# Counting masks in a threshold search: folds of 512 columns and sums of 512 values in place of 256

## The reference

```python
        S = jax.nn.relu(att[:, 0])
        S = S.at[..., 0].set(0.0)
        S = S * (1.0 - jnp.eye(T, dtype=S.dtype))
        S_shifted = jnp.concatenate([jnp.zeros((B, 1, T), S.dtype), S[:, :-1]], axis=1)
        FF = jnp.cumsum(S_shifted, axis=1)
        att = att - FF[:, None]
        ratio = _pruning_ratio(T)
        memory_budget = max(1, int(T * ratio))
        if ratio < 1.0:
            FF_mod = jnp.where(causal[None], FF, jnp.inf)
            sorted_idx = jnp.argsort(FF_mod, axis=-1)
            rank = jnp.argsort(sorted_idx, axis=-1)
            eff_k = jnp.minimum(memory_budget - 1, i + 1)
            keep = rank < eff_k[None, :, None]
```

## Time and profile before

| what | value |
|---|---|
| median of three runs | 2983.0 us (2960.94 to 2986.77) |
| span of the profiled execution | 2972.6 us |
| search stage, first mask to last settling | 144.5 to 394.8 us |
| PE busy in the span | 2648.6 us (89%) |
| DVE busy | 1845.0 us (62%) |
| ACT busy | 1787.0 us (60%) |
| POOL busy | 337.1 us (11%) |
| folds, L887 | 2176 matmuls, 238.4 us busy |
| counts, L897 | 416 activations, 157.6 us busy, and 416 reads of the accumulator, 81.9 us |

### The profile page before, as it was taken

How to read it: one execution, slowest core, us unless ns; L and a number is a source line. 1 busy time by engine, 2 the same in 40 slices (tenths; PEclk the granted TensorE clock), 3 DMA queues, 4 the chain that set the end, 5 groups by cost and what they waited for, 6 DMA issues and landing times. The chain is left out here.

```text
span 2972.6 us, 75835 instructions
## 1 busy us (share of the span) xinstructions
PE 2648.6 (89%) x31084; PEld 1645.1 (55%) x31084; DVE 1845.0 (62%) x5185; ACT 1787.0 (60%) x3488; POOL 337.1 (11%) x710
## 2 busy tenths in 40 slices
PE   8998978888888799999998889999999999897596
PEld 3386955666666563222212456676676667655355
DVE  5599978778787574100001657777777787753862
ACT  2375856555566527999998227666666666532331
POOL 1100033222222010000000100000000000016016
PEclk8998979999999899999999899999999999898598
DMA  3140001001110202110000010000000000203103
GB/s 95 42 67 1 2 2 17 17 17 17 17 17 10 54 1 66 54 45 1 1 1 1 17 40 2 7 7 7 2 7 7 7 2 2 79 29 47 33 13 59
DMA packets 84736, 67.84 MB, mean 23 GB/s; under 512 B 40584, under 2 KB 73496, under 8 KB 84008
## 3 DMA queue, kind: packets, MB, share of 16 engines
q1 hardware_dynamic: 75944, 56.70, 8.0%
q0 software_dynamic: 8448, 6.30, 1.6%
HBM read 47.21 MB, written 19.96 MB: 23 GB/s over the span
## 5 line engine op out<-in xcount | busy, mean ns | idle before, releaser
L1733 ACT ACTIVATE arena<-ps 128x1024 f32<-128x1024 f32 x512 | 474.1, 1300 | 25.9 <-PE ps L1683 24.1
L1184 DVE CUSTOM_DVE_ANT_0 arena<-ps,arena 128x1024 f32<-128x1024 f32 (+7 forms) x384 | 349.7, 930 | 107.8 <-PE ps L1060 91.9
L2111 DVE CUSTOM_DVE_ANT_0 arena<-ps,arena 128x512 f32<-128x512 f32 (+3 forms) x640 | 371.2, 643 | 26.7 <-PE ps L1975 25.9
L1136 ACT ACTIVATE arena<-ps 128x1024 f32<-128x1024 f32 (+3 forms) x320 | 275.4, 895 | 133.4 <-PE ps L1093 129.9
L2068 ACT ACTIVATE arena<-arena 128x1152 f32<-128x1152 f32 (+15 forms) x256 | 306.4, 1199 | 63.4 <-DVE arena L2111 63.4
L1975 PE MATMUL ps<-arena 64*128 64x512 f32 (+3 forms) x1280 | 270.4, 547 | 3.5 <-ACT arena L2044 1.1
L1694 PE MATMUL ps<-arena 128*32 128x512 f32 x2048 | 273.0, 604 | 0.0
L2006 PE MATMUL ps<-arena 128*64 128x128 f32 x4352 | 262.3, 275 | 0.0
L2006 PEld LDWEIGHTS ps<-arena 128*64 128x64 f32 x4352 | 235.3, 137 | 33.4 <-issue 28.7
L887 PE MATMUL ps<-arena 128*128 128x256 bf16 (+1 forms) x2176 | 238.4, 273 | 14.7 <-DVE arena L859 9.3
L1088 PE MATMUL ps<-arena 64*128 64x64 f32 x4352 | 218.0, 232 | 19.4 <-ACT arena L1136 11.5
(11 more groups left out here) (298 smaller groups left out, 4095.0 us busy)
## 6 DMA issues: line engine op xcount, KB each, us to landing
arena<-scr_q SPq DMA_DIRECT2D x256, 32.0 KB
scr_s<-scr_f SPq DMA_DIRECT2D x1, 4096.0 KB, 17.7
arena<-scr_k SPq DMA_DIRECT2D x32, 128.0 KB
arena<-by_head_k SPq DMA_DIRECT2D x16, 192.0 KB
arena<-scr_s SPq DMA_DIRECT2D x16, 192.0 KB, 2.6
arena<-by_head_q SPq DMA_DIRECT2D x28, 96.0 KB
by_head_k<-arena SPq DMA_DIRECT2D x5, 512.0 KB, 4.5
scr_x<-arena SPq DMA_DIRECT2D x2, 1024.0 KB, 5.4
```

Of the source, the lines that this page charges most:

```text
L1136: e.activation(turned_block(u, kc), src, ACT.Exp, scale=-1.0).then_inc(exped, 1)
L1184: e.tensor_tensor_reduce(scored_block(u, g)[:, lo:hi], PS[:, 1024 * (k % 2):1024 * (k % 2) + hi - lo], NF[t][:, lo:hi], -1.0, mxs[:, col - ...
L1733: e.activation(PTR[k % RS], PS[:, at(n):at(n) + 1024], ACT.Sigmoid, scale=float(1 / np.sqrt(8.0))).then_inc(weighed, 1)
L2111: e.tensor_tensor_reduce(slot(u, t, g)[:, lo:hi], PS[:, base(step) + 512 * g:base(step) + 512 * g + hi - lo], bias, -1.0, mxs[:, col - 1:c ...
```

## The change

PE folds a mask in pieces of 512 columns onto a whole PSUM bank. ACT sums all 512 values of the bank. The junk areas become four of 256 words in place of eight of 128, on the same 1024 words, and ACT waits for its own count four back in place of eight back.

```diff
-            junk = [reg(2048 + 128 * i, 128).bitcast(BF16) for i in range(8)]
+            junk = [reg(2048 + 256 * i, 256).bitcast(BF16) for i in range(4)]
@@ search_tensor
-                    for c0 in range(0, W, 256):
-                        c1 = min(c0 + 256, W)
+                    for c0 in range(0, W, 512):
+                        c1 = min(c0 + 512, W)
                         m = e.matmul(bank(n % 8, c1 - c0), IDB, tally[n % 7][:, c0:c1], start=(c0 == 0), stop=(c1 == W))
@@ search_scalar
-                    if n >= 8:
-                        w.wait_ge(counted, n - 7)
-                    e.activation(junk[n % 8], bank(n % 8, 256), ACT.Copy, accum_out=cnt[:, s:s + 1]).then_inc(counted, 1)
+                    if n >= 4:
+                        w.wait_ge(counted, n - 3)
+                    e.activation(junk[n % 4], bank(n % 8), ACT.Copy, accum_out=cnt[:, s:s + 1]).then_inc(counted, 1)
```

## The result

The changed kernel takes 2985.57 us in the median of 20 runs (2974.92 to 2997.03); the kernel before, over 20 runs, 2972.01 us (2960.94 to 2999.44). The ratio is 1.0039, with a 95% interval of 1.0021 to 1.0057: **slower by 0.4%**, small but clear. The forecast of 2997 us was built on the three runs then shown, whose median of 2983.0 lies 11 us above that of twenty.

What follows compares the result with a forecast made beforehand. PE was taken to bound the search before, ACT after, at 7.54 us a round in place of 7.10; 12.8 + 0.8 + 0.6 + 0.2 = +14.4 us on a median of 2983 gave 2997 us, range 2976 to 3014.

Steps and rivals of the forecast that it cites:

- The bound before: In the search, PE sets the round of 7.10 us: 6.93 of columns plus 2.5 ns for each of 68 matmuls.
- The count: ACT's sum of 512 folded values at L897: 0.365 + 0.215 = 0.58 us, 13 of them 7.54 us a round.
- The sum: All added time in the search: 12.8 + 0.8 + 0.6 + 0.2 = +14.4 us, or 0.48%.
- 29 rounds: Full-clock rounds of the search, 14 and 15, each going from 7.10 to 7.54 us: +12.8 us.
- the stretch between the halves: Search from 251.15 to 284.96 us: nothing while DVE sets the pace, then 0.6 us for counts queueing after half clock.
- counted already: After the half-clock stretch before 284 us, the later settling was taken as included elsewhere, leaving 0.6 us there.
- The size that can be told: Whole kernel: about 1% (30 us) can be told from no change; same 0.85, slower 0.12, faster 0.03.
- The base: Whole kernel before: median of 2983.0 us, to which 14.4 us was added for 2997 us.
- A, the clock: PE's granted clock falls in the search because PE waits each round; five half-clock rounds give 3029 us; chance 0.07.
- B, PE stays the bound: In the search a count costs under 0.540 us, so the round is PE's 7.02 us: 2981 us; chance 0.08.
- C, a stall: ACT stalls at each set in the search; with 0.5 us of stall a round of 8.06 us: 3013 us; chance 0.05.
- What would show each step: Signs in the search: 264 us long, 597 ns activations, PE gap some 0.5 us, L843 waits about 22 us, clock 1.00.

Runs made afterwards that it cites:

- without tile 3: Kernel before, with tile 3 left unfolded and its mask summed by ACT straight from its buffer, and four junk areas: a round of 6.885 us, ratio 0.9995.
- the second comparison: The changed kernel run again, against the kernel before on the same chip: median of 12 runs 2985.04 us, ratio 1.0036 (1.0011 to 1.0061).
- the padding: Four more small DVE operations, results unused, ahead of each settling of the first set; added to the changed kernel: a round of 7.521 us.
- the padded kernel before: Kernel before with four more small DVE operations, results unused, ahead of each settling of the first set: a round of 7.122 us.

## Why the prediction was right and where it was wrong

**The bound before: right.** PE's 7.10 us as 6.93 of columns plus 2.5 ns for each matmul gave 7.02 for folds of 512, 7.04 for 448 and 6.885 without tile 3; the runs have 7.026, 7.044 and 6.885. The 0.2 to 0.3 us that DVE was said to have left in a round of 7.10 are 0.28: its round is 6.82 us in the run where it is the bound.

**The count: right.** 0.58 us and a round of 7.54 were forecast from plain activations of the same widths; 0.5785 and 7.52 were measured. The Trainium skill, "ScalarE: Activation LUTs", section "What ACT_TABLE_LOAD costs", gives 0.833 ns an element, and the step from 480 to 512 columns agrees, 0.83. The estimate by its fixed cost and its overlap of neighbours, 0.52 us for a count of 512, does not fit: 0.5785 was measured.

**The sum: right, with one term too small.** In the trace: first round 7.93 in place of 7.16 us, +0.8 (forecast 0.8); 29 rounds +12.1 (12.8); the stretch between the halves, 254.37 to 289.08 in place of 251.15 to 284.96, +0.9 (0.6); the tail 3.47 in place of 3.25, +0.2 (0.2). Together +14.0 where +14.4 was forecast. The round, 7.52 in place of 7.54 us, makes 0.7 of the difference with the rounding of 7.10, and the middle gives 0.3 back. There I had counted only the queue of counts after the half-clock stretch and called the later settling "counted already". It is not. DVE's long products take the same time in both kernels, 251.15 to 276.98 us before and 254.37 to 280.21 after, 25.8 us; they start from one settling and end ahead of another, so the 0.2 us by which a wide count settles later are paid once more. The rows of the changed kernel:

```profile
286.62 0.60 ACT L897 ACTIVATE arena<-ps 128x512 bf16<-128x512 f32 x1
...
288.35 0.61 ACT L897 ACTIVATE arena<-ps 128x512 bf16<-128x512 f32 x1
```

Three steps of 0.58 us, and 0.73 from the last start to the settling at 289.08. In the kernel before, the same three steps took 0.39 each (283.29 to 284.46) and the settling followed 0.50 us later, at 284.96. Together that is 0.8 us; the other 0.1 is that the first of the four counts starts 6.41 us behind the settling at 280.21, where it was 6.31.

**The size that can be told: wrong.** This is the step that failed. The prediction said that about 1%, 30 us, is what a measurement of this kernel can tell from no change, and so gave "same" 0.85 and "slower" 0.12, although its own sum stood at +14.4 us. It was right that the change lies within 1%. But it took the spread of single runs, 26 us, for what a comparison of many runs can tell. With 20 runs of each kernel the interval is 0.18% to either side, about 5 us and not 30, and 1.0021 to 1.0057 excludes no change; so does the second comparison, 1.0011 to 1.0061. The mechanism and the sum held, and by them the outcome to name was "slower", by a little; the 0.80 on rounds of 7.3 to 7.9 us, 7 to 25 us of loss, belonged there. The chances also differ within themselves: a tenth of the forecast was said to lie beyond 1%, and 0.05 of it stands in the sum.

**The base: wrong.** The absolute time was 11.4 us too high, and 11.0 of it is the median of three runs, 2983.0, in place of 2972.0. The profiled span of 2972.6 lay nearer, and span plus sum, 2987.0, is within 1.5 us of the measured median. That is luck in part: a profiled execution is one run like any other, and that of the run with tiles 3 and 4 summed directly, repeated, took 2953.95 us where the median of its 12 was 2968.04. So is it luck that the medians differ by 13.6 us, as near to 14.4 as that: their interval is 5 us wide to either side. What bears the mechanism out is the search in the traces, 14.0 us longer.

**The rivals.** *A, the clock:* out. PE stood 0.32 us in each round and the granted clock was 1.00 in every stretch of full rounds. The Trainium skill, "TensorE: Matmul & The Clock Gate", section "A second HAM failure mode: psum-queue depth-cycling", tells of short idles between bf16 matmuls of 512 columns that made the clock swing. This trace does not agree: from 150 to 254 us and from 290 to 402 us, with folds of that form over eight banks, the clock stayed at 1.00. *B, PE stays the bound:* out at 512, but it is what happens at 448 columns. *C, a stall:* out by the padding, which cost the changed kernel nothing, and by ACT's record, which has no idle time in full rounds.

**What would show each step.** The signs came in but for two of their numbers. PE's gap in a round is 0.32 us in the record, not 0.5; the record has PE busy for 7.20 us where its matmuls need 7.03, so 0.2 of the gap is hidden. And the activations of 512 columns, forecast at 597 ns, are recorded with 0.60 us only at the start of a half, and with up to 1.52 later; the last section tells why that is no cost. L843's waits rose to 23.2 us, 22 forecast. The claim that nothing outside the search moves by more than 5 us held in the pair (3.4 and 0.7), but it held by luck: in the second trace of the changed kernel the part ahead was 12.3 us shorter than in the kernel before and the part behind 10.3 longer.

## What to carry to other kernels

Before work is handed from a full engine to one with room, set the three needs of a round side by side: here PE 7.10, DVE 6.82, ACT 4.75 us. The change took 0.08 from the first and put 2.8 on the last, and the crossing, some 466 columns by an estimate from the 0.365 us of a count and the slope of plain activations, lies between the runs of 448 and 480. It could be worked out before any run. The same room on ACT, spent on whole tiles that PE then need not fold, shortened the round by 0.28 us. And when a change is worth a few tenths of a per cent, take the base from many runs, and ask what many runs can tell before "no change" is forecast.

## What the runs showed of the hardware

**ACT's records grow while it is the bound.** In the changed kernel an activation of 512 columns is recorded with 0.60 us at the start of a long full stretch, and each one is some 8 ns longer than the one before, with starts 0.57 us apart, until 1.5 us are reached near 210 us. From there the records go up and down between 1.43 and 1.52, and one start in thirteen comes 0.64 us behind its neighbour.

```profile
149.48 0.62 ACT L897 ACTIVATE arena<-ps 128x512 bf16<-128x512 f32 x1
...
155.75 0.72 ACT L897 ACTIVATE arena<-ps 128x512 bf16<-128x512 f32 x1
...
241.73 1.52 ACT L897 ACTIVATE arena<-ps 128x512 bf16<-128x512 f32 x1
```

The ends are 0.579 us apart (eleven steps from 150.10 to 156.47 us) and agree with the round. At 480 columns the records grow too (mean 1069 ns), at 448, where PE is the bound, hardly (571). Means like 1209 and 820 ns above tell that ACT ran without a pause, not what an operation costs. Where the growth comes from stays open.

**The same code ahead of the search ran at very different clocks.** The stage that computes FF, unchanged in all these kernels, ran at granted clocks from 0.71 to 0.98 in the profiled executions, with PE busy nearly all the time. The stretch from 20 to 133 us, in the second run of the changed kernel and in the padded kernel before:

```profile
20.00:133.00 113.00, 108.77 (x274) 44.02 (x273) 61.31 (x83) 42.34 (x81) 18.44 (x48) 0.98 0.25 73
```

```profile
20.00:133.00 113.00, 113.00 (x211) 41.80 (x209) 43.21 (x58) 32.79 (x64) 14.22 (x42) 0.71 0.18 61
```

The first search began at 132.2 us; in the second it began at 160.3 us, where the kernel before had 144.5. In the kernel before the clock of that stretch was 0.86, in the changed one 0.89, which fits the 3.4 us by which its search began earlier. So a difference of 10 us between two spans of this kernel can come from this stage alone. It is not the only one: from the last settling to the end the traces take 2575 to 2588 us on one chip and 2598 to 2613 on the two others. The length of a round is the measure that tells a change in the search. Why the clock differs ahead of it from run to run stays open.
